# A two-layer graph network kernel: message stage skewed by a group, dense rows in 39 steps of 10, one batch of small operations a group, no fills

## The reference

```
xw = einsum('nf,rfg->rng', h, W)
out_j, out_i = xw[edge_type, src], xw[edge_type, dst]
logits = leaky_relu((out_i @ q + out_j @ k)[:, 0], 0.2)
alpha = segment_softmax(logits, dst)
h = relu(segment_sum(alpha[:, None] * out_j, dst) + b)
```

## Time and profile before

| | us |
|---|---|
| median of three runs | 1289.93 |
| the profiled execution | 1288.88 |
| its span | 1286.9 |
| PE busy | 813.2 (63%) |
| DVE busy | 843.5 (66%) |
| ACT busy | 602.7 (47%) |
| POOL busy | 697.9 (54%) |
| PE products with the relation matrices (L564) | 318.7 |
| ACT norms of dense rows (L660) | 311.6 |
| DVE masks (L1030) | 213.7 |
| POOL fills (L401) | 112.4 |

### The profile page before, as it was taken

The page is one execution under the profiler, slowest core; times in us unless marked ns, Lnnn a source line. Parts: engine busy times, 40 slices in busy tenths (PEclk is TensorE's granted clock), DMA queues, the critical chain, the costliest instruction groups (busy, mean ns, idle before and its releaser), DMA issues.

```text
span 1286.9 us, 12299 instructions
## 1 busy us (share of the span) xinstructions
PE 813.2 (63%) x3263; PEld 548.0 (43%) x3263; DVE 843.5 (66%) x2444; ACT 602.7 (47%) x1391; POOL 697.9 (54%) x911
## 2 busy tenths in 40 slices
PE   3425554445444432989999856768989999656400
PEld 2313333334323321545554446765445555455400
DVE  3666667776777764686777666436777777599910
ACT  1555556666666663234444423343444444355510
POOL 5778777887300006788889000277878400047875
PEclk9555556665665565989999977656989999775655
DMA  5944444344332223122221224322212111011110
GB/s 173 255 134 142 135 125 120 119 123 121 112 97 82 81 67 95 36 63 65 64 63 60 70 72 122 91 71 71 63 49 79 62 57 34 26 39 56 49 46 32
DMA packets 90868, 110.07 MB, mean 86 GB/s; under 512 B 14516, under 2 KB 66874, under 8 KB 90799
## 3 DMA queue, kind: packets, MB, share of 16 engines
q1 hardware_dynamic: 75119, 87.74, 22.9%
q0 software_dynamic: 15680, 21.55, 6.2%
HBM read 74.94 MB, written 44.89 MB: 93 GB/s over the span
## 4 chain that ended last, share of the span: by engine, by line
PE 35%; issue 17%; DVE 16%; POOL 12%; ACT 12%; SPq 4%; DMA 3%; POOLq 0%; DVEq 0%; ACTq 0%
PE ps_y L564 22%; POOL out L442 7%; ACT stage L660 5%; POOL xs L410 4%; PE ps_y L525 3%; ACT xd L670 3%; PE ps_y L526 3%; DVE ys L942 2%; PE ps_k L571 2%; ACT opT L630 2%; DVE xd L980 2%; PE ps_t L495 2%; DVE st L918 2%; SPq L308 2%; DVE work L1030 2%
## 5 line engine op out<-in xcount | busy, mean ns | idle before, releaser
L564 PE MATMUL ps_y<-work,wr 128*128 128x512 f32 (+1 forms) x784 | 318.7, 560 | 14.1 <-DVE work L1030 13.9
L660 ACT ACTIVATE stage<-stage,nm,rs 128x128 f32<-128x128 f32 x792 | 311.6, 480 | 23.3 <-DVE nm L868 23.3
L410 POOL DMA_INDIRECT xs<-x_table,posI x98 | 132.0, 1346 | 187.6 <-DMA x_table<-xd 154.6
L1030 DVE SCALAR_TENSOR_TENSOR work<-typB,opT 128x896 f32<-128x896 uint8 x196 | 213.7, 1091 | 24.4 <-PE ps_y L564 24.4
L564 PEld LDWEIGHTS ps_y<-work,wr 128*128 128x128 f32 x784 | 141.7, 192 | 187.7 <-issue 97.7
L410 POOL DMA_INDIRECT xs<-h_table,posI x98 | 121.7, 1241 | 152.3 <-issue 152.3
L442 POOL DMA_INDIRECT out<-xd,outI x98 | 107.0, 1092 | 153.5 <-ACT xd L670 124.0
L867 DVE RECIPROCAL rs<-sd 128x12 f32<-128x12 f32 (+2 forms) x109 | 23.6, 216 | 244.8 <-ACT sd L650 221.7
L630 ACT ACTIVATE opT<-ps_t 128x896 f32<-128x896 f32 x56 | 51.0, 911 | 275.9 <-issue 203.4
L495 PE MATMUL ps_t<-identS,ys 128*128 128x128 f32 x98 | 24.4, 427 | 160.4 <-ACT opT L630 160.4
L401 POOL MEMSET pause<- 128x224 uint8 x392 | 112.4, 287 | 19.4
(11 more groups left out here) (187 smaller groups left out, 1274.6 us busy)
## 6 DMA issues: line engine op xcount, KB each, us to landing
stage<-in_x SPq DMA_DIRECT2D x65, 384.0 KB, 3.6
out<-stage SPq DMA_DIRECT2D x65, 384.0 KB, 2.3
x_table<-xd SPq DMA_DIRECT2D x14, 448.0 KB, 4.8
h_table<-work SPq DMA_DIRECT2D x14, 448.0 KB, 3.3
work<-in_src SPq DMA_DIRECT2D x13, 448.0 KB, 6.2
ys<-in_edge_attr SPq DMA_DIRECT2D x6, 896.0 KB, 11.7
sameB<-same_rows SPq DMA_DIRECT2D x42, 112.0 KB, 3.5
typB<-typ_rows SPq DMA_DIRECT2D x28, 112.0 KB, 3.5
```

What stands on the lines that cost most here:

```text
L410: nc.gpsimd.indirect_dma_start(out=buf[:, t, :], out_offset=None, in_=table, in_offset=bass.IndirectOffsetOnAxis(ap=idx[:, t:t + 1], axis= ...
L564: mm = pe.matmul(ps_y[:, u, lo:hi], wr[:, r, :], rows, start=(r == 0), stop=(r == R - 1))
L660: ins = a.activation(slot(c)[:, r, :], slot(c)[:, r, :], ACT.Identity, bias=nm[:, h, n:n + 1], scale=rs[:, h, n:n + 1])
L1030: STT(work[:, n % 2, :], typB[:, m % 2, :], float(r), opT[:, g % 2, :], ALU.is_equal, ALU.mult).then_inc(m_mask[j], 1)
```

## The change

Five edits.

- **Dense rows.** BR goes from 6 to 10: 39 slots of 10 rows and a remainder, SLOTS from 4 to 3. Three steps stand ahead of the message stage as before; the message stage has one step a group (14), the first product stage one in front and one in each group, the second one in front and one in each of seven groups; the remainder's second norm follows in its eighth group instead of after the loop.
- **One batch a group.** The statistics of the dense rows (20), of `xd` (7) and of `xs` (7) go into one array of W = 34; one batch of sums, one Sqrt, one reciprocal and one product serve them. Before, there were four batches a group.
- **Skew.** PE multiplies the messages of group g+1 behind the turn back of group g, which now goes to `ps_s` and `ps_k`; `positions(g+1)` stands at the end of the group. On DVE a group begins with the running sums. ACT normalizes the rows of group g-1 while DVE works on group g; it has one more round. SP stores the `x1_table` rows ahead of the bulk step; the edge features are loaded two groups at a time during the stage and no longer all at the start; ACT does the first messages before bulk steps 1 and 2.
- **No fills** after the gathers on POOL.
- **Query scores of layer 2** stand inside the sums loop, a group late, on PE and ACT. The 8 `hot` compares move from the start to behind the message stage, and a few buffers share memory.

```
-    BR = 6
+    BR = 10
     BC = N // P // BR
     BREM = N - BC * BR * P
     assert BREM <= P and (N // P) % BR == 0
-    SLOTS = 4
+    SLOTS = 3
...
     K_A = 3
...
-    HEAD = [2, REST_STEPS - 2]
-    K_H = [K_A + 2 * NG, K_A + 2 * NG + HEAD[0] + NG]
-    K_M = [K_H[j] + HEAD[j] for j in range(2)]
-    RESTS = 7
-    PAUSE = 224
+    K_H = [K_A + NG, K_A + NG + 1 + NG]
+    K_M = [K_H[0] + 1, K_H[1] + 1]
+    K_E = [K_M[0] + NG, BC + 1]
+
+    W = 2 * BR + 2 * G
+    XD, XS = 2 * BR, 2 * BR + G
+    assert K_E[0] == K_H[1] and 0 < K_E[1] - K_M[1] < NG
...
+        def back(t):
+            return ps_s[:, t * P:(t + 1) * P] if t < 4 else ps_k[:, (t - 4) * P:(t - 3) * P]
...
+            sp.wait_ge(p_step, 1)
+            src_spread(1)
...
+            for k in range(1, K_A):
+                bulk_step(k)
+            edges(1)
...
+            for g in range(NG + 1):
+                if 0 < g < NG - 1:
                     sp.wait_ge(p_step, g + 1)
                     src_spread(g + 1)
-                bulk_step(K_A + 2 * g)
-                sp.wait_ge(a_scan, g + 1)
-                same_spread(g + 2)
-                bulk_step(K_A + 2 * g + 1)
-                sp.wait_ge(f_rows[0], g + 1)
-                sp.dma_start(grp(x1_rows, g), grp(xd, g)).then_inc(tab_out[0][g % 2], 16)
+                if g % 2 and g // 2 + 2 < NG // 2:
+                    edges(g // 2 + 2)
+                if g < NG:
+                    sp.wait_ge(a_scan, g + 1)
+                    same_spread(g + 2)
+                if g:
+                    sp.wait_ge(f_rows[0], g)
+                    sp.dma_start(grp(x1_rows, g - 1), grp(xd, g - 1)).then_inc(tab_out[0][(g - 1) % 2], 16)
+                    bulk_step(K_A + g - 1)
...
-                rest(RESTS)
...
+            def turn_xs(g):
                 pe.wait_ge(xs_in[0][g % 2], (g // 2 + 1) * (16 * G))
                 turn_group(xs, g)
+
+            def messages(g):
                 if g % 2 == 0:
                     pe.wait_ge(ea_in[g // 2], 16 if g < NG - 2 else 48)
                 turn_group(ys, g)
                 pe.wait_ge(a_Ts, turned[0])
                 if g:
+                    pe.wait_ge(a_ys, g)
+                for lo, hi in HALVES:
+                    pe.matmul(ps_y[:, 0, lo:hi], m_node, opT[:, 0, lo:hi], start=True, stop=False)
+                    mm = pe.matmul(ps_y[:, 0, lo:hi], m_edge, opT[:, 1, lo:hi], start=False, stop=True)
+                mm.then_inc(a_msg, 1)
+
+            def rows_scores(g):
+                pe.wait_ge(f_rows[0], g + 1)
+                turn_group(xd, g)
+                pe.wait_ge(x_used, min(g + 2, NG))
+                query_scores(0, g, a_Ts, turned[0])
+
+            pe.wait_ge(wqk_s, 1)
+            pe.wait_ge(c_r, 1)
+            positions(0)
+            turn_xs(0)
+            messages(0)
+            pe.wait_ge(prol_d, 1)
+            for g in range(NG):
+                if g < NG - 1:
+                    turn_xs(g + 1)
+                if g:
                     pe.wait_ge(x_used, g)
...
-                if g:
-                    pe.wait_ge(f_rows[0], g)
-                    turn_group(xd, g - 1)
-                    n = turned[0]
+                if g >= 2:
+                    pe.wait_ge(f_qs[0], g - 1)
                 pe.wait_ge(a_scan, g + 1)
                 for t in range(G):
-                    mm = pe.transpose(ps_y[:, 0, t * P:(t + 1) * P], ys[:, g * G + t, :], ident)
+                    mm = pe.transpose(back(t), ys[:, g * G + t, :], ident)
                 mm.then_inc(x_T, 1)
+                if g < NG - 1:
+                    messages(g + 1)
                 if g:
-                    query_scores(0, g - 1, a_Ts, n)
-            pe.wait_ge(f_rows[0], NG)
-            turn_group(xd, NG - 1)
-            query_scores(0, NG - 1, a_Ts, turned[0])
+                    rows_scores(g - 1)
+                if g < NG - 1:
+                    positions(g + 1)
+            rows_scores(NG - 1)
...
+                        if j == 0:
+                            query_scores(1, g - 1, g_act[0], g)
 
             for j in range(2):
                 relation_products(j)
                 sums(j)
-                if j == 0:
-                    for g in range(NG):
...
+            bulk_step(0, second=False)
+            act.wait_ge(c_r, 1)
+            turned_out(opT[:, 0, :])
+            turned_out(opT[:, 1, :])
+            messages_out(0)
+            for k in range(1, K_A):
+                bulk_step(k)
+
+            for g in range(NG + 1):
+                k = K_A + g - 1
+                h = k % 2
+                if g:
+                    act.wait_ge(b_rs, k + 1)
+                    norm_rows(xd, g - 1, h, XD, f_rows[0])
+                if g < NG - 1:
+                    act.wait_ge(a_msg, g + 1)
+                    turned_out(opT[:, 0, :])
+                if g:
+                    bulk_norm(k, 1, range(BR // 2))
+                if g < NG - 1:
+                    turned_out(opT[:, 1, :])
+                if g:
+                    bulk_norm(k, 0)
+                if g < NG - 1:
+                    messages_out(g + 1)
                 if g:
                     turned_out(cols_of(ys, g - 1))
+                    bulk_norm(k, 1, range(BR // 2, BR))
+                    norm_rows(xs, g - 1, h, XS, a_norm)
                     query_scores_out(0, g - 1)
+                if g < NG:
+                    act.wait_ge(b_sum, k + 2)
+                    root(k + 1, 0, W).then_inc(b_sd, 1)
...
+                    if K_M[j] + g < K_E[j]:
+                        bulk_step(K_M[j] + g)
                     products_out(g)
-                if j == 1:
-                    bulk_step(BC + 1, first=False)
+                    if j == 1 and K_M[j] + g == K_E[j]:
+                        bulk_step(BC + 1, first=False)
...
-                dve.wait_ge(xs_in[0][u], (g // 2 + 1) * (16 * G))
-                stats7(xs, g, 0).then_inc(a_sum, 1)
-                search(g, lambda n: bulk_first(kA, range(n, n + 1)))
-                bulk_first(kA, range(4, BR))
-                bulk_shift(kA)
-                bulk_second(kA)
-                bulk_sums(kA)
-                dve.wait_ge(a_sd, g + 1)
-                row_scales(0, u).then_inc(a_rs, 1)
-                bulk_scales(kA)
+                k = K_A + g
+                h = k % 2
                 dve.wait_ge(a_ys, g + 1)
                 running_sums(g, g, a_scan)
+                row_stats(xs, g, h, XS)
+                bulk_first(k)
+                dve.wait_ge(x_T, g + 1)
+                dve.wait_ge(xd_in[u], (g // 2 + 1) * (16 * G))
+                for t in range(G):
+                    c = g * G + t
+                    T.of(STT(xd[:, c, :], back(t), rcpC[:, c:c + 1], xd[:, c, :], ALU.mult, ALU.add))
+                T.wait()
+                dve.sem_inc(x_used, 1)
+                row_stats(xd, g, h, XD)
+                search(g, lambda n: bulk_shift(k) if n == 0 else bulk_second(k, range((n - 1) * 4, min(n * 4, BR))))
+                sums(k, 0, W).then_inc(b_sum, 1)
...
+                dve.wait_ge(b_sd, k + 1)
+                scales(k, 0, W).then_inc(b_rs, 1)
+
+            for r in range(R):
+                T.of(TS(hot[:, r, :], rcp[:], float(r), None, ALU.is_equal))
...
-                    bulk_piece(0, k)
+                    piece = bulk_piece if k < K_E[j] else lambda n, k: None
+                    piece(0, k)
                     for r in range(1, R):
                         n = g * (R - 1) + r - 1
                         if n >= 2:
                             dve.wait_ge(m_used[j], n - 1)
                         STT(work[:, n % 2, :], typB[:, m % 2, :], float(r), opT[:, g % 2, :],
                             ALU.is_equal, ALU.mult).then_inc(m_mask[j], 1)
-                        bulk_piece(r, k)
+                        piece(r, k)
                     if g == 2:
                         own_queries()
-                if j == 1:
-                    bulk_step(BC + 1, first=False)
+                    if j == 1 and k == K_E[j]:
+                        bulk_step(BC + 1, first=False)
```

More of the change, by code:

```diff
@@ new lines, in bulk_norm, with bulk_step @@
+            def bulk_norm(k, half, rows=range(BR)):
+                h, c, done = k % 2, k - half, (b_norm1, b_norm2)[half]
+                for r in rows:
+                    n = half * BR + r
+                    ins = a.activation(slot(c)[:, r, :], slot(c)[:, r, :], ACT.Identity,
+                                       bias=nm[:, h, n:n + 1], scale=rs[:, h, n:n + 1])
+                if rows[-1] == BR - 1:
+                    ins.then_inc(done, 1)
+            def bulk_step(k, first=True, second=True):
@@ L849, in _ @@
             dve.sem_inc(deg_r, 1)
-            T.step(v.tensor_copy(typF, typR))
-            for r in range(R):
-                T.of(TS(hot[:, r, :], typF, float(r), None, ALU.is_equal))
             dve.wait_ge(mix_s, 2)
```

212 lines of the change are left out of this document (62 added, 150 removed).

## The result

The changed kernel takes 1363.66 us (median of four runs, 1357.62 to 1365.06) against 1289.81: the ratio is 1.0565, interval 1.0533 to 1.0597. It is 5.65% slower; I had forecast 1169. The profiled execution took 1365.06 us with a span of 1363.3.

The account below looks back on a forecast made before the run. Two stages were taken as bound by waits (message stage, 30.0 us a group) and two product stages by PE. The stretches summed to 1166.5, plus 2.0 and 1.0, giving 1169 us; range 1130 to 1222.

Parts of the forecast that it names:

- POOL: Gathers from x in the message stage: without fills about 253 us, done near 265, last asked for near 326.
- The start: Stretch ahead of the message stage: 86.6 us against 85.1, plus 1.5, with messages(0) ahead of bulk steps 1 and 2.
- Message stage: Thirteen groups at 20.0 us instead of 30.0, 260.0 in all, a gain of 129.9; bounds 18.7 to 21.7 a group.
- rival A: PE keeps the high clock: message groups of 18.7, a sums loop of 67, 1138 us in all; chance 0.15.
- The slots: Dense-row reload in the message stage with three slots: store plus load of 640 KB take 7.9 us, landing in time.
- Product stages: Both layers' masked products: DVE bounds loaded groups at 17.1 us instead of 14.8; stages of 259.6 and 234.0 us.
- The last stretch: From layer 2's first product to the end: 410.1 us predicted against 397.7 in the unchanged kernel.
- Rival C: Product stages lose the high clock as PE stands for masks: groups of 29.7, 1295 to 1434 us; chance 0.04.
- Sums loop: Loop taking in layer 2's query scores: 5.3 us a group, a quarter at low clock, 81 against 73.9; bounds 67 to 119.
- From loop to first product: Last table store to first product: 31.3 us in layer 1 instead of 40.8, 26.5 in layer 2, a gain of 38.6.
- The sum itself: Whole kernel: stretches add to 1166.5 us, plus 2.0 around the span and 1.0 to the median, said as 1169.

Follow-up runs that it names:

- e1: The changed kernel with the seven fills put back behind every seven gathers (all 42 groups), nothing else: 1201.67 us, ratio 0.932.
- after: The changed kernel as predicted and measured, with all five edits and no fills, against the kernel without them: 1363.66 us, ratio 1.0565.
- e16: The changed kernel with one fill of 150 bytes a partition behind every gather from x, none behind the later ones: 1166.05 us, ratio 0.9046.
- before: The kernel without the change, with seven fills behind every seven gathers: 1289.81 us.

## Why the prediction was wrong, step by step

**The fills: the step that failed.** Under "POOL" I let them go at "No price", beyond 2.5 us between two gather groups, and asked only whether the gathers would be done in time. They were (260.5 against "near 265"). I priced a removed pause on POOL by what POOL gains and not by what the pause gives to the others. So "The start ... plus 1.5" was -2 with the fills (82.6 in e1) and +210 without. No rival of mine had this mechanism.

**Message stage.** Predicted 20.0 a group, measured 18.25 on average (18.16 in most), under my lower end of 18.7. (DVE's terms there add to 17.95 and not 17.7, which leaves the 20.0 between the bounds where it was.) ACT's order in after (one round):

```profile
373.75 0.90 ACT L640 ACTIVATE opT<-ps_t 128x896 f32<-128x896 f32 x1
374.55 3.95 ACT L665 ACTIVATE stage<-stage,nm,rs 128x128 f32<-128x128 f32 x10
378.40 0.99 ACT L696 ACTIVATE ys<-ps_y,bcol 128x896 f32<-128x896 f32 x1
```

The message copy waits for nothing (6.00 before): the eight products take 3.3 us with 1.00 of the clock granted, as rival A had it, and not the middle that I took. The slots were no trouble: a store of 640 KB took 2.9 us and, in e16, a load 4.1, together 7.0 where I took 7.9. By the fit of the Trainium skill ("DMA: Bandwidth & Descriptors", Anatomy of one DMA) an estimate of the sum is 7.0 as well; but it splits it evenly, and the page gives the fit for DMAs that GpSimd issues, while these come from SP.

In after all gathers had landed before the stage began. In e16 POOL works beside it: the first seven groups take 18.2 to 18.7 even so, but from the eighth on most wait for gathered rows (up to 22.9), and the stage takes 252.2 us. The prediction asked whether POOL's 253 us fit in front of its last use near 326. They do, but at 1.36 us a gather, and with 29 that took 1.1 to 2.56 us instead of 0.95, beside a DVE at work, POOL ends at 305.5, just behind the stage's need.

**Product stages.** 17.1 a group predicted, 17.15 measured, PE waiting 0.2 to 0.8 for masks; then the group with the refills (24.9, +7.8), which I had not seen, and 17.5 behind it. The first stage is 3.1 over the forecast: the refills cost 7.8 in one group, where in before they cost 4.3 in two late ones (17.37 and 16.57). The last stretch is 7.1 under: the unloaded groups take 14.32, where I left them at the 14.8 of before (3.5 for seven), and the group behind that with the own queries grew by 1.0 (16.97 to 17.99) and not 2.3; the rest I did not trace.

Rival C did not come. The sentence of the Trainium skill that I set beside it ("TensorE: Matmul & The Clock Gate", A second HAM failure mode) would have the clock oscillate with a gap at each mask; the granted clock averaged 0.95 over the first stage, softmax included, so gaps of 0.2 to 0.8 us did no harm here.

**Sums loop.** The mechanism was right, the size off: I gave a quarter of the groups the low clock. (The terms of a group at the high clock add to 4.1 there, not 4.3.) A steady group takes 7.47 us with PE never idle for long:

```profile
867.64 3.33 PE L618 MATMUL ps_y<-r_lg,identS 98*128 98x128 f32 x14
870.77 1.70 PE L626 MATMUL ps_t<-identS,ys 128*128 128x128 f32 x7
872.26 2.99 PE L495 MATMUL ps_k<-wqk,ys 128*128 128x8 f32 x14
875.11 3.33 PE L618 MATMUL ps_y<-r_lg,identS 98*128 98x128 f32 x14
```

Alpha takes 3.33 where it took 1.73, and 2.99 for a block of scores is near its 3.13 there. The granted clock was 0.50 over these two groups and 0.61 over the loop, with PE 94% busy: scores and alpha were both at the low clock for most of it. The loop cost 90.4, not 76.5 (from its first alpha on 94.9, not 81), inside the bounds of 67 to 119.

**From loop to first product.** 31.5 and 27.7 against 31.3 and 26.5: right.

**The sum itself.** e16 is the changed kernel with gathers slowed to a step that lets the others run, and it takes 1166.05 where I said 1169. By stretch (same cuts):

```profile
0.00:81.70 81.70, 32.97 (x138) 24.21 (x139) 42.08 (x166) 31.45 (x68) 63.98 (x111) 0.77 0.52 157
81.70:333.90 252.20, 143.76 (x805) 111.88 (x801) 225.09 (x731) 217.86 (x518) 199.80 (x297) 0.75 0.58 179
...
644.60:734.60 90.00, 82.70 (x464) 81.70 (x463) 49.91 (x59) 27.66 (x41) 0.00 (x0) 0.63 0.34 84
```

That it agrees so well is in part chance: 13.5 us too little for the sums loop and 6 for the first product stage and the stretch behind the loop, against 8 too much for the message stage, 8 for the last stretch and 5 for the start.

## What to carry to other kernels

A pause that looks useless may be what lets other engines run: before taking waits or fills from a queue of indirect DMAs, look at what the others do while these are issued without a break, and set the step between them, not only their end. Where several engines show waits of 50 us and more for work that ended long before, with "remote" or "issue" as releaser, look for the one engine that never rests. And deal such pauses out evenly: one of 0.24 us behind every gather did what 2.4 us behind seven did, for 36 us less.

## What the runs showed of the hardware that I had not expected

- Indirect gathers of 128 rows issued by POOL each 1.25 to 1.30 us hold up PE, ACT and DVE for up to 92 us at a time, with the DMA share at 0.07 in one such stretch and the rate at 51 to 53 GB/s in another. At 1.36 to 1.42 us, evenly spaced, they do not. The Trainium skill ("SBUF — State Buffer", SBUF: two separate sides) says that PE and ACT never wait for another engine's port; a port between DVE and POOL is then no explanation.
- What is late is the engines' signals: in after a semaphore update of PE is recorded 81 us behind the end of its product, and updates of DVE come 1.4 us apart until 284.8, 23 us behind the last gather's last packet (261.8), then seven within 0.15 us. That engines and gathers share a path for such signals, and that it fills up, fits this, but is not shown; why the gathers hold it, and whether the recording of the trace takes a part in it, no run here tells.
- The limit lies between 1.30 and 1.36 us for even gathers; 1.32 (alternating gaps) gave 1286 to 1350 us in four executions of one program.
- POOL copies that ran back to back kept one DVE operation with two SBUF inputs from ending for 8.88 us, and two for 12.34.
